# Expert tiles of a routed MLP: gate and up products ordered high rows first, and a tile's result copied from PSUM by ScalarE

## Chip, cores and metric

One core of one Trainium2 chip runs the whole program. The metric is the device time of one execution in microseconds (us). A change of less than about 0.2% cannot be told from no change here.

## What is computed

The model has two layers. Layer 0 is an attention and a dense MLP whose weights are made from splines; layer 1 is a selective scan followed by a mixture of experts. The change touches the expert part alone, which in the reference is:

```python
# D = 512, M = 192, 32 experts, 8 per token, T = 2048 tokens
routing_weights = jax.nn.softmax(x2d @ gate_kernel, axis=-1)
routing_weights, selected_experts = jax.lax.top_k(routing_weights, TOP_K)
routing_weights = routing_weights / jnp.sum(routing_weights, axis=-1, keepdims=True)
...
w0 = jax.lax.ragged_dot(sorted_inputs, gate_proj, group_sizes)
w1 = jax.lax.ragged_dot(sorted_inputs, up_proj, group_sizes)
inter = jax.nn.silu(w0) * w1
expert_out = jax.lax.ragged_dot(inter, down_proj, group_sizes)
...
output = jnp.einsum('BKE,BK->BE', per_token, routing_weights)
x = x + output
```

## The kernel before

Blocks A, B and C (up to about 1235 us) are attention, dense MLP, scan and routing. Block D (`block_d`) is the expert part. The 16384 token and expert pairs are sorted by expert and cut into tiles of 128 rows; an expert has 4 or 5 tiles, and block D works through some 144 tiles in order. The five engines each run their own loop over the tiles, unrolled by 8 (VectorE by 4), and meet only at semaphores. Every f32 operand is cut into a high part (rounded to fp32r) and a low part (the rest), and a product is made of high by high, high by low and low by high.

What happens to tile t:

- POOL (GpSimd) gathers its 128 rows from HBM with an indirect DMA (`D_rows<-rows_d`, L1458), four tiles ahead: in its turn for tile t it first issues the gather of tile t+4, and then the scatter of tile t (L1491), an indirect DMA that adds the tile's result to `out`. Two experts can add to one row of `out`. So at the first tile of each expert POOL waits, ahead of the scatter, until all scatters before it have landed. After every fourth tile it also copies four columns of indices (L1455).
- PE turns the rows (`turn_rows`, L1296, four transposes into one bank, `pT`). ScalarE copies that bank to `xT_hi` (`turn`, L1363, semaphore `xT_first`). VectorE then takes bank minus `xT_hi` as `xT_lo` (`turn_lo`, L1412, semaphore `xT_sb`).
- PE makes gate and up (`gate_up`, L1300 to L1302, 12 products for four chunks of 128 rows: for each chunk `xT_hi` by `W_gu_hi`, `xT_hi` by `W_gu_lo`, `xT_lo` by `W_gu_hi`).
- ScalarE makes silu (L1367), VectorE multiplies by up and by the token's share (`weigh`, L1405 and L1407, semaphore `inner_done`), PE turns that (L1336), VectorE cuts it in high and low (L1428, L1430), PE makes the five down products (L1352 to L1356), VectorE copies the sum from PSUM to `ysb` (`D_y`, L1444, semaphore `y_sb`), and POOL scatters it.

PE's turn for tile t is: the transposes L1336 of tile t, `gate_up` of tile t+1, `turn_rows` of tile t+2, the down products of tile t. Time from one L1336 to the next is called a PE turn below.

Once for each expert, three experts ahead (`SPLIT_AHEAD`), the weights are cut too: ScalarE makes `W_gu_hi` (L1370) and `W_d_hi` (L1210, L1211) at the end of its turn for the expert's first tile, and VectorE makes `W_gu_lo` (L1436) and `W_d_lo` (L1450) in its turn for the second tile, `W_gu_lo` ahead of `weigh` and `W_d_lo` at the end. Both have two SBUF inputs. When they are done SP loads the next expert's weights.

Of the kernel before, what the change touches and what calls it, by code (L numbers as in the profile page):

```python
# [16 lines left out]
ds = bass.ds  # L17
# [5 lines left out]
ACT = mybir.ActivationFunctionType  # L23
AX = mybir.AxisListType.X

P = 128
NB, L, D = 4, 512, 512
DC = 256
KC = D // P
# [12 lines left out]
GUW, MR = 2 * M, M - P  # L42
UNROLL = 8
# [3 lines left out]
NSLOT, NRAW = 4, 2  # L47
# [1175 lines left out]
def block_d(nc, a, X, ident, bank, meta, idx_all, W, rows_d):  # L1223

    with ExitStack() as s:
# [4 lines left out]
        xT_hi, xT_lo = ([sb(f"xT_{h}{i}", [P, KC * P], F32R) for i in range(2)] for h in ("hi", "lo"))  # L1230
        sil, inner = [sb(f"sil{i}", [P, M]) for i in range(2)], [sb(f"inner{i}", [P, 2 * P]) for i in range(2)]
        iT_hi, iT_lo = ([sb(f"iT_{h}{i}", [P, 2 * P], F32R) for i in range(2)] for h in ("hi", "lo"))
        ysb = sb("y", [P, UNROLL, D])
        first_counts = sb("first_counts", [1, 4])
        pT, piT, pgu, py = bank[0], bank[1], [bank[2], bank[3]], [bank[4], bank[5]]
# [3 lines left out]
        xT_ps, xT_first, xT_sb, gu_ps, sil_done, inner_done, iT_ps, iT_first, iT_sb, y_ps, y_sb = (  # L1239
            sem(n) for n in ("xT_ps", "xT_first", "xT_sb", "gu_ps", "sil_done", "inner_done", "iT_ps", "iT_first", "iT_sb", "y_ps", "y_sb"))  # L1240
# [3 lines left out]
        def field(eng, f, tile, hi):  # L1244

            return eng.value_load(meta[0:1, f, ds(tile, 1)], min_val=0, max_val=hi)
# [6 lines left out]
        def fetch(eng, regs, f, tile):  # L1253

            eng.load(regs, meta[0:1, f, ds(tile, len(regs))])  # L1255
# [5 lines left out]
        def ring(eng, e, ahead, size):  # L1261

            return eng.snap((e + ahead) & (size - 1), min_val=0, max_val=size - 1)
# [28 lines left out]
        @block.tensor  # L1292
        def _(pe):
            def turn_rows(i):
                for k in range(KC):
                    mm = pe.transpose(pT[:, k * P:(k + 1) * P], rows[i][:, k * P:(k + 1) * P], ident[:, :])  # L1296
                mm.then_inc(xT_ps, 1)

            def split_products(ps, hi, lo, whi, wlo, n, last):
                pe.matmul(ps, hi, whi, start=n == 0, stop=False)  # L1300
                pe.matmul(ps, hi, wlo, start=False, stop=False)  # L1301
                return pe.matmul(ps, lo, whi, start=False, stop=last)  # L1302

            def gate_up(buf, i, meanwhile=None):
                for k in range(KC):
                    if k == 2 and meanwhile:
                        meanwhile()
                    x, w = slice(k * P, (k + 1) * P), slice(k * GUW, (k + 1) * GUW)
                    whi, wlo = (t[:, ds(buf, 1), w].rearrange("p o n -> p (o n)") for t in (W.gu_hi, W.gu_lo))
                    mm = split_products(pgu[i % 2][:, 0:GUW], xT_hi[i % 2][:, x], xT_lo[i % 2][:, x], whi, wlo, k, k == KC - 1)  # L1310
                mm.then_inc(gu_ps, 1)

            pe.wait_ge(ld_rows[0], 16)
            turn_rows(0)
            buf = field(pe, SLOT, 0, NSLOT - 1)
            pe.wait_ge(W.gu_split, 1)
            pe.wait_ge(xT_sb, 1)
            gate_up(buf, 0)
            pe.wait_ge(ld_rows[1], 16)
            turn_rows(1)  # L1320


            experts, go = registers(pe, "pe_experts", UNROLL), pe.alloc_register("pe_go")
            fetch(pe, [go], GO, 0)
            fetch(pe, experts[0:HALF], EXPERT, 0)
            with pe.Fori(0, NTILE // UNROLL) as q:
                with pe.If(held(pe, go, 1) > 0):
                    ahead = {0: lambda: fetch(pe, experts[HALF:], EXPERT, q * UNROLL + HALF),
                             2: lambda: fetch(pe, [go], GO, q * UNROLL + UNROLL),
                             HALF: lambda: fetch(pe, experts[:HALF], EXPERT, q * UNROLL + UNROLL)}  # L1330
                    for i in range(UNROLL):
                        t = q * UNROLL + i
                        expert, next_expert = (held(pe, experts[n % UNROLL], NE - 1) for n in (i, i + 1))
                        pe.wait_ge(inner_done, t + 1)
                        for c in range(2):
                            mm = pe.transpose(piT[:, c * P:(c + 1) * P], inner[i % 2][:, c * P:(c + 1) * P], ident[:, :])  # L1336
                        mm.then_inc(iT_ps, 1)

                        pe.wait_ge(xT_sb, t + 2)
                        pe.wait_ge(W.gu_split, next_expert + 1)  # L1340
                        gate_up(ring(pe, next_expert, 0, NSLOT), i + 1, ahead.get(i))

                        j = (i + 2) % UNROLL
                        pe.wait_ge(ld_rows[j], q * 16 + (16 if i + 2 < UNROLL else 32))
                        turn_rows(j)
                        pe.wait_ge(iT_sb, t + 1)
                        pe.wait_ge(W.d_split, expert + 1)
                        buf = ring(pe, expert, 0, NSLOT)
                        first, last = slice(0, P), slice(P, 2 * P)
                        hi_a = W.d_hi[:, ds(buf, 1), 0:D].rearrange("p o n -> p (o n)")  # L1350
                        lo_a, both_b = (W.d_lo[:, ds(buf, 1), c * D:(c + 1) * D].rearrange("p o n -> p (o n)") for c in range(2))
                        pe.matmul(py[i % 2][:, :], iT_hi[i % 2][:, first], hi_a, start=True, stop=False)  # L1352
                        pe.matmul(py[i % 2][:, :], iT_lo[i % 2][:, first], hi_a, start=False, stop=False)
                        pe.matmul(py[i % 2][:, :], iT_hi[i % 2][:, first], lo_a, start=False, stop=False)
                        pe.matmul(py[i % 2][:, :], iT_hi[i % 2][:, last], both_b, start=False, stop=False)
                        mm = pe.matmul(py[i % 2][:, :], iT_lo[i % 2][:, last], both_b, start=False, stop=True)  # L1356
                        mm.then_inc(y_ps, 1)

        @block.scalar
        def _(act):  # L1360
            def turn(n, i):
                act.wait_ge(xT_ps, n + 1)
                act.activation(xT_hi[i % 2][:, :], pT[:, :], ACT.Copy).then_inc(xT_first, 1)  # L1363

            def silu(n, i):
                act.wait_ge(gu_ps, n + 1)
                act.activation(sil[i % 2][:, :], pgu[i % 2][:, 0:M], ACT.Silu).then_inc(sil_done, 1)  # L1367

            def split_hi(raw, buf):
                act.activation(slot(W.gu_hi, buf), slot(W.raw_gu, raw), ACT.Copy).then_inc(W.gu_hi_done, 1)  # L1370
                W.split_down_hi(act, raw, buf).then_inc(W.d_hi_done, 1)

            turn(0, 0)
            silu(0, 0)
            turn(1, 1)
            splits, go = registers(act, "act_splits", UNROLL), act.alloc_register("act_go")
            fetch(act, [go], GO, 0)
            fetch(act, splits, SPLITS, 0)
            with act.Fori(0, NTILE // UNROLL) as q:
                with act.If(held(act, go, 1) > 0):  # L1380
                    to_split = [held(act, r, 1) for r in splits]
                    for i in range(UNROLL):
                        t = q * UNROLL + i
                        if i == 2:
                            fetch(act, [go], GO, q * UNROLL + UNROLL)
                        if i == HALF:
                            fetch(act, splits, SPLITS, q * UNROLL + UNROLL)
                        silu(t + 1, i + 1)
                        turn(t + 2, i + 2)
                        with act.If(to_split[i] > 0):  # L1390
                            e = field(act, EXPERT, t, NE - 1 - SPLIT_AHEAD)
                            act.wait_ge(W.ld, (e + SPLIT_AHEAD + 1) * 32)
                            act.sem_inc(passed)
                            split_hi(ring(act, e, SPLIT_AHEAD, NRAW), ring(act, e, SPLIT_AHEAD, NSLOT))

        @block.vector
        def _(v):
# [24 lines left out]
            with v.Fori(0, NTILE // HALF) as q:  # L1422
                with v.If(held(v, go, 1) > 0):
                    code = [held(v, r, NE - 1 + CODE_SHARE * NE) for r in codes]
                    for i in range(HALF):
                        t = q * HALF + i
# [4 lines left out]
                        with v.If(code[i] > CODE_SHARE - 1):  # L1431
                            e1 = v.snap(code[i] >> CODE_BITS, min_val=1, max_val=NE - SPLIT_AHEAD)
                            raw, buf = ring(v, e1, SPLIT_AHEAD - 1, NRAW), ring(v, e1, SPLIT_AHEAD - 1, NSLOT)
# [6 lines left out]
                            fetch(v, codes, CODE, q * HALF + HALF)  # L1440
                        if i == 2:
                            fetch(v, [go], GO, ((q + 1) >> 1) * UNROLL)
                        v.wait_ge(y_ps, t + 1)
                        v.tensor_copy(ysb[:, ds(t & (UNROLL - 1), 1), :].rearrange("p o n -> p (o n)"), py[i % 2][:, :]).then_inc(y_sb, 1)  # L1444
                        with v.If(code[i] > CODE_SHARE - 1):
                            e1 = v.snap(code[i] >> CODE_BITS, min_val=1, max_val=NE - SPLIT_AHEAD)
                            raw, buf = ring(v, e1, SPLIT_AHEAD - 1, NRAW), ring(v, e1, SPLIT_AHEAD - 1, NSLOT)
# [101 lines left out]
```

## Time and profile before

| what | value |
|---|---|
| median of three runs | 1982.0 us (1979.49 to 1982.53) |
| profiled execution | 1981.46 us, span 1979.3 us |
| PE busy | 1614.6 us, 82% of the span |
| VectorE (DVE) busy | 1205.5 us, 61% |
| POOL busy | 1132.2 us, 57% |
| ScalarE (ACT) busy | 787.1 us, 40% |
| block D, 1236 to 1966 us | 730 us: PE 633.9, DVE 465.6, POOL 412.4, ACT 215.2 us busy |

Busy time counts an engine's own work. PE's matmuls overlap, so that their summed durations say little about how fast they follow each other; the starts in the timeline do. Waits on a semaphore are shown as idle time with what ended it.

### The profile page before, as it was taken

Reading aid. Unit: us, or ns where it says so; the run is one execution under the profiler, and the core shown is the slowest. Engines: PE = TensorE matmul, PEld = TensorE weight load, DVE = VectorE, ACT = ScalarE, POOL = GpSimd, SP = SyncE. Lnnn points to the kernel's source line nnn. Section 1 sums busy time; section 2 is a strip of 40 time slices with the busy share of each in tenths; the row PEclk is TensorE's granted clock in tenths of the full one; section 3 lists DMA queues with packets and bytes.
Section 4 is the critical chain, followed back from the end, with each engine's and each line's share of the span. In section 5 each row is a group of like instructions: output and inputs, shape, how many; then the busy total and the mean of one; then the engine's idle time right before and its main releaser. Section 6 shows DMA issues by size and latency. Waiting matters only on the chain. (4 is left out here: it accounts for less than half of the span.)

```text
span 1979.3 us, 24590 instructions
## 1 busy us (share of the span) xinstructions
PE 1614.6 (82%) x5970; PEld 997.9 (50%) x5971; DVE 1205.5 (61%) x2202; ACT 787.1 (40%) x1131; POOL 1132.2 (57%) x573
## 2 busy tenths in 40 slices
PE   5887758999999999899993553888888888888896
PEld 2333333444444444444441542777777777776775
DVE  3655675566565655565656568566656666665664
ACT  3344435555555555555553610332222232223221
POOL 0211128888888878887981221466555556555564
PEclk9878878999999999999996655999999999999998
DMA  3122226667666766675768421677767677776665
GB/s 118 75 75 75 90 98 181 136 139 157 165 137 135 157 156 144 135 163 127 147 123 248 121 74 55 150 169 178 168 157 164 160 157 159 183 178 150 152 116 97
DMA packets 78787, 275.73 MB, mean 139 GB/s; under 512 B 11266, under 2 KB 12195, under 8 KB 66963
## 3 DMA queue, kind: packets, MB, share of 16 engines
q0 software_dynamic: 42496, 150.37, 38.6%
q1 hardware_dynamic: 36242, 124.79, 20.0%
q8 instruction: 21, 0.34, 0.1%
q14 instruction: 28, 0.22, 0.0%
HBM read 148.22 MB, written 126.90 MB: 139 GB/s over the span
## 5 line engine op out<-in xcount | busy, mean ns | idle before, releaser
L690 DVE TENSOR_TENSOR_SCAN B_E<-bank,B_E 128x512 f32<-128x512 f32 x256 | 306.5, 1212 | 205.4 <-ACT bank L645 199.2
L1491 POOL DMA_INDIRECT out_x<-D_y,D_rows x144 | 253.0, 1757 | 224.0 <-issue 117.1
L733 POOL TENSOR_TENSOR B_E<-B_E,B_Cb 128x2048 f32<-128x2048 f32 x64 | 291.9, 4561 | 109.7 <-DVE B_E L690 109.7
L727 POOL TENSOR_TENSOR B_E<-B_dtu,B_Bb 128x2048 f32<-128x2048 f32 x64 | 292.3, 4567 | 31.6 <-DMA B_Bb<-bc_d 31.6
L1300 PE MATMUL bank<-W_gu_hi,D_xT_hi 128*128 x580 | 213.8, 369 | 62.5 <-DVE D_xT_lo L1412 60.7
L606 PE MATMUL bank<-B_Wd,B_inter 128*128 128x512 f32 x512 | 230.7, 597 | 33.3 <-DVE X L684 32.4
L596 PE MATMUL bank<-hT,B_Wg 128*128 128x512 f32 x512 | 235.5, 603 | 22.3 <-DVE B_inter L679 21.2
L596 PE MATMUL bank<-hT,B_Wu 128*128 128x512 f32 x512 | 230.2, 592 | 0.0
L645 ACT ACTIVATE bank<-B_dtv,negA 128x512 f32<-128x512 f32 x256 | 171.8, 687 | 136.4 <-DVE B_E L690 135.7
L1367 ACT ACTIVATE D_sil<-bank 128x192 f32<-128x192 f32 x145 | 47.9, 330 | 446.7 <-PE bank L1302 446.6
L1458 POOL DMA_INDIRECT D_rows<-rows_d,D_source x148 | 159.1, 1075 | 98.5 <-issue 92.0
L1301 PE MATMUL bank<-W_gu_lo,D_xT_hi 128*128 x580 | 197.3, 340 | 0.0
L1302 PE MATMUL bank<-W_gu_hi,D_xT_lo 128*128 x580 | 197.0, 340 | 0.0
L1405 DVE SCALAR_TENSOR_TENSOR D_inner<-D_sil,D_rows,bank 128x128 f32<-128x128 f32 x145 | 50.3, 347 | 200.3 <-ACT D_sil L1367 200.1
L606 PEld LDWEIGHTS bank<-B_Wd,B_inter 128*128 128x128 f32 x512 | 92.8, 190 | 155.7 <-issue 91.9
L596 PEld LDWEIGHTS bank<-hT,B_Wg 128*128 128x128 f32 x512 | 97.0, 193 | 142.4 <-issue 140.6
L1300 PEld LDWEIGHTS bank<-W_gu_hi,D_xT_hi 128*128 128x128 f32 x580 | 110.6, 191 | 99.3 <-issue 98.5
L596 PEld LDWEIGHTS bank<-hT,B_Wu 128*128 128x128 f32 x512 | 97.4, 190 | 122.3 <-issue 122.3
L1363 ACT ACTIVATE D_xT_hi<-bank 128x512 fp32r<-128x512 f32 x146 | 87.4, 599 | 111.9 <-PE bank L1296 98.8
L1412 DVE TENSOR_TENSOR D_xT_lo<-bank,D_xT_hi 128x512 fp32r<-128x512 f32 x146 | 100.0, 685 | 32.0 <-ACT D_xT_hi L1363 32.0
L1296 PE MATMUL bank<-ident,D_rows 128*128 128x128 f32 x584 | 89.8, 277 | 35.3 <-DMA D_rows<-rows_d,D_source 35.2
L364 POOL TENSOR_SCALAR A_one<-A_ex 128x2048 f32<-128x2048 f32 x4 | 21.5, 5367 | 169.3 <-ACT A_ex L279 169.3
(244 smaller groups left out, 2838.5 us busy)
## 6 DMA issues: line engine op xcount, KB each, us to landing
y_d<-B_E POOLq DMA_DIRECT2D x64, 1024.0 KB, 8.1
W_raw_gu<-in_wgu SPq DMA_DIRECT2D x32, 768.0 KB, 6.1
B_Bb<-bc_d SPq DMA_DIRECT2D x32, 512.0 KB, 5.4
B_Cb<-bc_d SPq DMA_DIRECT2D x32, 512.0 KB, 4.0
W_raw_d<-in_wd SPq DMA_DIRECT2D x32, 512.0 KB, 7.5
rows_d<-C_row SPq DMA_DIRECT2D x4, 1090.0 KB, 5.1
X<-in_x SPq DMA_DIRECT2D x4, 1024.0 KB, 9.0
dt_d<-A_dtv SPq DMA_DIRECT2D x4, 1024.0 KB, 3.9
```

The costliest lines, as they stand in the source:

```text
L596: mm = pe.matmul(ps[:, :], W[:, k, ch * P:(ch + 1) * P], hT[:, k, tb * L:(tb + 1) * L], start=k == 0, stop=k == KC - 1)
L606: mm = pe.matmul(Yb[t % 2][:, :], inter[jj % 2][:, ch, t * P:(t + 1) * P], Wd[w][:, ch, :], start=ch == 0, stop=ch == 1)
L645: act.activation(dA[m % 2][:, :], dtv[:, c, :], ACT.Exp, scale=negA[:, c, n:n + 1]).then_inc(dA_done, 1)
L690: v.tensor_tensor_scan(E[:, s % NR, c, :], dA[m % 2][:, :], E[:, s % NR, c, :], 0.0, ALU.mult, ALU.add).then_inc(s_done, 1)
L727: g.tensor_tensor(E[:, s % NR, :, :], dtu[b % 2][:, :, :], spread(Bb[jj % 2][:, s % 2, :]), ALU.mult).then_inc(dbu_done, 1)
L733: g.tensor_tensor(E[:, s % NR, :, :], E[:, s % NR, :, :], spread(Cb[jj % 2][:, s % 2, :]), ALU.mult).then_inc(prod_done, 1)
L1300: pe.matmul(ps, hi, whi, start=n == 0, stop=False)
L1301: pe.matmul(ps, hi, wlo, start=False, stop=False)
L1302: return pe.matmul(ps, lo, whi, start=False, stop=last)
L1412: v.tensor_tensor(xT_lo[i % 2][:, :], pT[:, :], xT_hi[i % 2][:, :], ALU.subtract).then_inc(xT_sb, 1)
L1458: g.indirect_dma_start(rows[i], None, rows_d[:, :], bass.IndirectOffsetOnAxis(ap=source[i // HALF][:, i % HALF:i % HALF + 1].bitcast(U32), ...
L1491: g.indirect_dma_start(a["out"], bass.IndirectOffsetOnAxis(ap=rows[i][:, ROW - 1:ROW].bitcast(U32), axis=0), ysb[:, i, :], None, compute_o ...
```

## The change

`gate_up` makes the eight products with `xT_hi` first, all four chunks, and then the four with `xT_lo`. It waits for `xT_first` ahead of the first eight and for `xT_sb` only ahead of the last four. The reading of registers that stood in the middle of it (`meanwhile`) stands between the two halves. The copy of a tile's result from PSUM leaves VectorE's turn, where it stood behind `turn_lo`, and goes to ScalarE's turn, behind `turn` and ahead of the cutting of weights.

```diff
-            def split_products(ps, hi, lo, whi, wlo, n, last):
-                pe.matmul(ps, hi, whi, start=n == 0, stop=False)
-                pe.matmul(ps, hi, wlo, start=False, stop=False)
-                return pe.matmul(ps, lo, whi, start=False, stop=last)
-
-            def gate_up(buf, i, meanwhile=None):
+
+            def gate_up(buf, i, tile, meanwhile=None):
+                ps = pgu[i % 2][:, 0:GUW]
+
+                def operands(k, x, w):
+                    return x[i % 2][:, k * P:(k + 1) * P], w[:, ds(buf, 1), k * GUW:(k + 1) * GUW].rearrange("p o n -> p (o n)")
+                pe.wait_ge(xT_first, tile + 1)
                 for k in range(KC):
-                    if k == 2 and meanwhile:
-                        meanwhile()
-                    x, w = slice(k * P, (k + 1) * P), slice(k * GUW, (k + 1) * GUW)
-                    whi, wlo = (t[:, ds(buf, 1), w].rearrange("p o n -> p (o n)") for t in (W.gu_hi, W.gu_lo))
-                    mm = split_products(pgu[i % 2][:, 0:GUW], xT_hi[i % 2][:, x], xT_lo[i % 2][:, x], whi, wlo, k, k == KC - 1)
+                    pe.matmul(ps, *operands(k, xT_hi, W.gu_hi), start=k == 0, stop=False)
+                    pe.matmul(ps, *operands(k, xT_hi, W.gu_lo), start=False, stop=False)
+                if meanwhile:
+                    meanwhile()
+                pe.wait_ge(xT_sb, tile + 1)
+                for k in range(KC):
+                    mm = pe.matmul(ps, *operands(k, xT_lo, W.gu_hi), start=False, stop=k == KC - 1)
                 mm.then_inc(gu_ps, 1)
...
-                        pe.wait_ge(xT_sb, t + 2)
                         pe.wait_ge(W.gu_split, next_expert + 1)
-                        gate_up(ring(pe, next_expert, 0, NSLOT), i + 1, ahead.get(i))
+                        gate_up(ring(pe, next_expert, 0, NSLOT), i + 1, t + 1, ahead.get(i))
...
                         turn(t + 2, i + 2)
+                        act.wait_ge(y_ps, t + 1)
+                        act.activation(ysb[:, i, :], py[i % 2][:, :], ACT.Copy).then_inc(y_sb, 1)
                         with act.If(to_split[i] > 0):
...
-                        v.wait_ge(y_ps, t + 1)
-                        v.tensor_copy(ysb[:, ds(t & (UNROLL - 1), 1), :].rearrange("p o n -> p (o n)"), py[i % 2][:, :]).then_inc(y_sb, 1)
```

PE's queue in a tile's turn before, from the transposes of `inner` to the second chunk of `gate_up` (REGISTER_ALU and ISA rows are the sequencer's work on addresses, and the semaphore a row waits for is in brackets):

```order
L1336 MATMUL bank<-ident,D_inner 128x128 [waits D_inner_done]
L1336 MATMUL bank<-ident,D_inner 128x128
L1339 REGISTER_ALU
L1340 REGISTER_ALU [waits D_xT_sb]
L1300 REGISTER_ALU [waits W_gu_split]
L1300 ISA
L1300 MATMUL bank<-W_gu_hi,D_xT_hi 128x384
L1301 REGISTER_ALU
L1301 MATMUL bank<-W_gu_lo,D_xT_hi 128x384
L1302 MATMUL bank<-W_gu_hi,D_xT_lo 128x384
```

The same place after the change, with the end of `gate_up` behind the "...":

```order
L1338 MATMUL bank<-ident,D_inner 128x128 [waits D_inner_done]
L1338 MATMUL bank<-ident,D_inner 128x128
L1341 REGISTER_ALU
L1305 REGISTER_ALU [waits W_gu_split]
L1307 REGISTER_ALU [waits D_xT_first]
L1307 ISA
L1307 MATMUL bank<-W_gu_hi,D_xT_hi 128x384
L1308 REGISTER_ALU
L1308 MATMUL bank<-W_gu_lo,D_xT_hi 128x384
...
L1255 TENSOR_LOAD meta
L1313 MATMUL bank<-W_gu_hi,D_xT_lo 128x384 [waits D_xT_sb]
```

The wait for `D_xT_sb` has moved behind eight products and the register load; the number of products and of sequencer rows ahead of the first product is what it was.

ScalarE's queue in a tile's turn after the change, from silu to the cutting of the gate and up weights:

```order
L1368 ACTIVATE D_sil<-bank 128x192 [waits D_gu_ps]
L1363 REGISTER_ALU
L1364 ACTIVATE D_xT_hi<-bank 128x512 [waits D_xT_ps]
L1391 REGISTER_ALU
L1392 ACTIVATE D_y<-bank 128x512 [waits D_y_ps]
L1393 COMPARE_AND_BRANCH
L1246 ISA
L1246 TENSOR_LOAD meta
L1246 ISA x2
L1395 ISA
L1371 REGISTER_ALU [waits W_ld]
```

The two rows with L1391 and L1392 are new; ahead of the branch there stood nothing between it and the copy to `D_xT_hi`. The register load `L1246` and all of the weight cutting now come behind a wait for PE's down products.

## Rows read from the trace of the kernel before

**Rows 1.** Window, block D; busy (count) of PE, PEld, DVE, ACT, POOL; granted clock.
```profile
1236.00:1966.00 730.00, 633.89 (x3328) 523.03 (x3328) 465.60 (x928) 215.18 (x382) 412.42 (x321) 0.99 0.70 158
```

**Rows 2.** Waits in 1236 to 1966 us: total, times, longest.
```profile
PE bank L1300 <- DVE D_xT_lo L1412: 60.7, 139, 1.6
PE bank L1296 <- DMA D_rows<-rows_d,D_source: 25.8, 18, 2.9
```

**Rows 3.** Timeline of a plain tile: start us, us, engine, line, names.
```profile
1606.10 0.68 DVE L1412 TENSOR_TENSOR D_xT_lo<-bank,D_xT_hi 128x512 fp32r<-128x512 f32 x1
1606.23 0.44 PE L1336 MATMUL bank<-ident,D_inner 128*128 128x128 f32 x2
...
1606.70 0.68 DVE L1444 COPY D_y<-bank 128x512 f32 x1
1607.12 0.44 PE L1300 MATMUL bank<-W_gu_hi,D_xT_hi 128*128 x1 [0.44 <-DVE D_xT_lo L1412]
...
1608.22 1.58 POOL L1491 DMA_INDIRECT out_x<-D_y,D_rows  x1 [1.75 <-DVE D_y L1444]
...
1609.31 0.60 PE L1296 MATMUL bank<-ident,D_rows 128*128 128x128 f32 x4
...
1610.95 0.44 PE L1336 MATMUL bank<-ident,D_inner 128*128 128x128 f32 x2
```

**Rows 4.** Timeline behind a long wait for rows.
```profile
1423.29 2.40 POOL L1491 DMA_INDIRECT out_x<-D_y,D_rows  x1 [3.01 <-issue]
...
1428.00 1.01 POOL L1458 DMA_INDIRECT D_rows<-rows_d,D_source  x1 [2.11 <-issue]
...
1435.19 1.12 PE L1296 MATMUL bank<-ident,D_rows 128*128 128x128 f32 x4 [2.41 <-DMA D_rows<-rows_d,D_source]
...
1438.23 0.39 PE L1336 MATMUL bank<-ident,D_inner 128*128 128x128 f32 x2
...
1438.38 0.42 PE L1300 MATMUL bank<-W_gu_hi,D_xT_hi 128*128 x1
...
1442.19 0.44 PE L1336 MATMUL bank<-ident,D_inner 128*128 128x128 f32 x2
```

**Rows 5.** Groups of instructions by line, 1236 to 1966 us.
```profile
L1363 ACT ACTIVATE D_xT_hi<-bank 128x512 fp32r<-128x512 f32 x146 | 87.4, 599 | 111.9 <-PE bank L1296 98.8
L1211 ACT ACTIVATE W_d_hi<-W_raw_d x30 | 18.9, 629 | 0.4
```

**Rows 6.** One line, L1436: durations, first and last start.
```profile
L1436 DVE TENSOR_TENSOR W_gu_lo<-W_raw_gu,W_gu_hi x30: 1757/1758/1761, 1249.3 to 1901.0; - x30
```

**Rows 7.** Timeline of an expert's four tiles around its first scatter.
```profile
1327.92 1.59 POOL L1491 DMA_INDIRECT out_x<-D_y,D_rows  x1 [0.81 <-DVE D_y L1444]
...
1330.73 1.49 ACT L1370 ACTIVATE W_gu_hi<-W_raw_gu  x1 [0.63 <-issue]
...
1333.49 1.76 DVE L1436 TENSOR_TENSOR W_gu_lo<-W_raw_gu,W_gu_hi  x1 [0.35 <-issue]
...
1333.72 2.98 POOL L1491 DMA_INDIRECT out_x<-D_y,D_rows  x1 [2.91 <-issue]
...
1336.88 1.22 DVE L1450 TENSOR_TENSOR W_d_lo<-W_raw_d,W_d_hi  x1
1337.01 1.96 POOL L1458 DMA_INDIRECT D_rows<-rows_d,D_source  x1 [0.30 <-DVE D_y L1444]
...
1344.45 0.66 PE L1296 MATMUL bank<-ident,D_rows 128*128 128x128 f32 x4 [0.64 <-DMA D_rows<-rows_d,D_source]
...
1348.04 1.59 POOL L1491 DMA_INDIRECT out_x<-D_y,D_rows  x1 [1.00 <-DVE D_y L1444]
```

**Rows 8.** Timeline of another expert's first scatter.
```profile
1465.54 1.49 ACT L1370 ACTIVATE W_gu_hi<-W_raw_gu  x1 [1.19 <-issue]
1467.35 1.58 POOL L1491 DMA_INDIRECT out_x<-D_y,D_rows  x1 [3.05 <-issue]
1467.60 1.76 DVE L1436 TENSOR_TENSOR W_gu_lo<-W_raw_gu,W_gu_hi  x1 [0.69 <-ACT W_gu_hi L1370]
```

More of the change, by code:

```diff
@@ L1316, in _ @@
             pe.wait_ge(W.gu_split, 1)
-            pe.wait_ge(xT_sb, 1)
-            gate_up(buf, 0)
+            gate_up(buf, 0, 0)
             pe.wait_ge(ld_rows[1], 16)
```

## The prediction

> **What bounds the kernel now.** I read the windows first. Block D takes 730 us, and PE, busy 634 us of them, is the fullest engine at full clock (0.99) [rows 1]; only this block is changed. Then the waits. PE waits for two things: `xT_lo` from VectorE, 139 times, 60.7 us in all, and gathered rows, 18 times, 25.8 us [rows 2]. So there are two limits, and I followed each in the timeline.
>
> The first is PE's own turn. In a plain tile it is 1610.95 - 1606.23 = 4.72 us. `turn_lo` ends at 1606.78, `gate_up` starts at 1607.12, 0.89 us after L1336 [rows 3], and the engine is idle 0.44 us of that. At 1438.23 rows had been late, so that `xT_lo` was long there: `gate_up` starts 0.15 us after L1336, and the turn is 1442.19 - 1438.23 = 3.96 us [rows 4].
>
> The second is a loop that runs once per expert through POOL. Take S1 at 1327.92 (the last scatter of the old expert) and S2 at 1333.72 (the first of the new one): 5.80 us, the time S1 needs to land. S2 takes 2.98 us where an undisturbed one takes 1.59, because `W_gu_lo` runs on VectorE from 1333.49 to 1335.25: S2 ends 1.45 us after it. The gather behind S2 starts at 1337.01, inside `W_d_lo` (1336.88 to 1338.10), and takes 1.96 us against 1.01. Its rows land 7.4 us after its start, and PE had waited 0.64 us for them at 1344.45; the down products behind them feed the scatter at 1348.04, the next S1 [rows 7, 4]. That is 20.12 us for four tiles, where PE alone would need 4 x 4.72 plus about 0.5 for the turn that `W_gu_lo` delays, 19.4. The loop and PE's work are nearly equally long. Where the index copy falls between S2 and the gather, the gather starts 4.71 us after S2 (1423.29 to 1428.00), PE waits 2.41 us, and the cycle is some 22.3 us [rows 4]; by the numbers of the tiles at which experts start in the timeline (modulo 4) this is so in 9 of 29 cycles.
>
> `W_gu_lo` runs 30 times, from 1249.3 to 1901.0 [rows 6]: 29 cycles of 22.47 us with 129 tiles, 4.45 a cycle.
>
> **The change, part by part.**
>
> (a) The early start of `gate_up`. `xT_hi` is ready 0.9 us before `xT_lo`, always ahead of L1336, so the wait goes. But the rows of PE's queue between L1336 and the first product stay, and the sequencer stands at `inner_done` until VectorE is through. From `xT_lo`'s end to the first product these rows now take 0.34 us [rows 3]; the bound below is 0.15, where the sequencer had run ahead [rows 4]. I take 0.40, nearer the plain tile: a saving of 0.49 a turn, 4.72 to 4.23. The bound is 0.74, 3.98. Twelve products take 1609.31 - 1607.12 = 2.19 us [rows 3], the eight high ones so 1.46, in which `xT_lo` is ready: its wait costs nothing.
>
> (b) The copy of the result. VectorE loses 144 copies of 0.68 us [rows 3]. The nearest form on ScalarE, also 128x512 from PSUM, takes 0.599 [rows 5]; the last down product stands right ahead of the next L1336 in PE's queue, and I put its end 0.15 us behind that one's start (an estimate; matmuls overlap). So the copy is done at 0.15 + 0.05 + 0.60 = 0.8 us of the turn, against 1.15 (1607.38 - 1606.23 [rows 3]) for VectorE. In a plain turn ScalarE is idle then; nothing is delayed. In the loop this is worth about 0.25 us a cycle.
>
> (c) In the turn in which weights are cut, ScalarE's work comes later. `W_gu_hi` starts 0.63 us behind the end of the instruction ahead [rows 7], now the copy: at 0.8 + 0.63 = 1.4 us of the turn instead of 0.2. It ends at 2.9, the two parts of `W_d_hi` (0.62 and 0.63) at 4.2 [rows 7, 5], and silu of the next tile, due at 2.8, waits for it. `W_gu_lo` starts 0.57 behind `W_gu_hi`'s end when it waits for it (1467.03 to 1467.60 [rows 8]): 3.5 to 5.25. `weigh` follows, and this turn becomes about 5.8 us, where it was 5.3. So PE alone needs 5.8 + 3 x 4.23 = 18.5 us for four tiles.
>
> (d) What becomes of the loop? In [rows 7] S2 started 0.23 us after `W_gu_lo` and stood until it ended. In [rows 8] S2 started 0.25 us before it and took 1.58: whichever starts first is not held up. The Trainium skill (SBUF — State Buffer, Who interferes with whom) says the same: a VectorE instruction with two SBUF inputs contends with GpSimd's reads, and the order of issue decides who blocks; by that rule the moved copy, which reads PSUM, never held POOL up. Here the order can turn over. S1 starts at 0.8 + 0.84 = 1.64 us of its turn (0.84 from `D_y`'s end at 1607.38 to its scatter at 1608.22 [rows 3]), S2 5.8 to 5.9 us later, which is 3.3 us of the following turn after 4.23 are taken off; `W_gu_lo` starts at 3.5. S2 is first by 0.2 us, less than these numbers are sure to. If S2 is first, it ends 1.4 us sooner than now, the gather is 2.3 us sooner done, and the loop falls to about 17.6, below PE's 18.5: PE bounds most experts. With the index copy behind S2 it is about 19.8. If `W_gu_lo` is first, the gather is done 1.75 + 1.05 + 0.9 behind it as now or 0.5 sooner, and the loop is 20.12 - 0.25 - 0.3 = about 19.55, with the index copy 22.3.
>
> The sum over 29 cycles of 4.45 tiles. S2 first: 18.5 + 0.45 x 4.23 + 9/29 x 1.3 = 20.8, a gain of 1.65 a cycle, 48 us. `W_gu_lo` first: 19.55 + 1.9 + 9/29 x 2.8 = 22.3, a gain of 0.15, 4 us. Ahead of the first cutting and behind the last there are 15 tiles more; POOL's drains bound most, and I take 4 us. With S2 first in two of three experts: 0.67 x 48 + 0.33 x 4 + 4 = 37 or 38. From the profiled 1981.46 that is 1944; the median, 1982.0, gives the same to 1 us.
>
> **The rivals.** *One: `W_gu_lo` meets every S2.* For it: it does in nearly all experts now, and my margin is 0.2 us. Gain 4 + 4: 1974, or up to 1980 if rows land later under the denser traffic (DMA share is 0.70 already [rows 1]). *Two: PE gets the whole 0.74 us*, the sequencer runs ahead, and S2 is first everywhere: 5.8 + 3 x 3.98 = 17.7 for four tiles, 17.7 + 1.8 + 9/29 x 2.1 = 20.2 a cycle, 29 x 0.6 = 17 us beyond the full gain of 48 + 4: 1912 or, with 3 us at the ends, 1909. Against it: the wait at `inner_done` ends just as the down products do. With 3.98 S2 also comes 0.25 later in its turn, beside `W_gu_lo`, so this needs luck twice. *Three, slower.* A PE that finishes sooner waits longer for the same rows. Behind the wait of 2.41 us its clock was low: four transposes took 1.12 us in place of 0.66, and L1336 came 3.04 us after their start where 1.64 is usual [rows 4, 7, 3]: the lower of the two levels, 1.4 us in the loop itself. If rival one holds and PE's waits of 1 us grow to 2.4 in more than 6 of 29 cycles (8 / 1.4), the gain of 8 is gone; in 21 of them, counting off the ones that have it now, it is 1974 + 30 = 2004. Against it: the plain cycle's wait would be 19.55 - 18.5 = 1.05 us. *Four: the delayed silu costs more than its 0.5 us*, because transposes of later rows queue behind it; that is the same loss by another way, inside the range of rival one.
>
> **How the numbers follow.** S2 first in most experts, forecast 1944 (own range 1928 to 1962): 0.45. Rival one, 1974 (1964 to 1982): 0.25. Rival two, 1905 to 1926: 0.13. Slower, to 2004: 0.13. A remainder of 0.04 on either side. The range that leaves out no more than 2 in 10: 1912 to 1984. Faster by over 0.2% (about what a measurement can tell, below 1978): 0.45 + 0.13 + 0.19 of rival one = 0.77. Within 0.2%: 0.09. Slower: 0.14.
>
> **What would show it.** (a) No wait of the first product for VectorE, and plain turns of 4.2 us from L1336 to L1336; 4.0 is rival two. (b) `D_y` on ScalarE, about 0.60. (c) `W_gu_hi` 1.4 us into its turn, and a turn of 5.8. (d) The durations of the scatters: now most expert starts show 1.8 to 3.1 us; near 1.58 in two thirds says S2 first, 3.0 in all says rival one. In rival three the down products behind waits for rows last twice as long. I am wrong if rows land much later than 7.4 us, or if the first scatter's place in the turn is off by more than 0.2 us.

## The result, and the profile after

The kernel after takes 1948.5 us (median of 4, 1946.3 to 1950.6) against 1980.7 us before on the same chip (median of 4): ratio 0.984, 95% interval 0.982 to 0.986. The forecast was 1944. The profiled execution took 1950.59 us with a span of 1948.8.

Block D's window, with the columns of [rows 1]:

```profile
1236.00:1966.00 730.00, 634.18 (x3332) 535.87 (x3331) 380.69 (x784) 295.41 (x526) 402.02 (x326) 0.96 0.71 159
```

VectorE is down from 466 to 381 us and ScalarE up from 215 to 295, as the moved copy should do. The window reaches past the end of this shorter run (span 1948.8), so the clock is better compared over 1236 to 1910 us: it is 0.96, where the kernel before has 0.98 (short parts of the block are at the lower level, 1.2 GHz, the rest at 2.4). The waits of the same stretch, with the columns of [rows 2], and behind them PE's wait for `D_inner` in the kernel before:

```profile
DVE W_gu_lo L1439 <- ACT W_gu_hi L1371: 63.1, 30, 2.6
PE bank L1338 <- DVE D_inner L1410: 50.8, 31, 2.1
PE bank L1296 <- DMA D_rows<-rows_d,D_source: 17.7, 10, 9.6
PE bank L1307 <- ACT D_xT_hi L1364: 0.9, 1, 0.9
```
```profile
PE bank L1336 <- DVE D_inner L1407: 5.6, 12, 0.8
```

The 139 waits of PE for `xT_lo` are gone. The wait for `D_inner`, 5.6 us in all before, is now about 1.6 us once per expert. The wait for rows seems to fall from 25.8 to 17.7 us, but 9.6 of the 17.7 is the one at the block's start. The kernel before has that one too, 9.4 us at 1234.5, which is just outside the window of [rows 2]. Like for like it is 18 waits and 25.8 us before, 9 waits and 8.1 us after. A plain tile, as in [rows 3]:

```profile
1612.02 0.44 PE L1338 MATMUL bank<-ident,D_inner 128*128 128x128 f32 x2
1612.18 0.60 ACT L1392 ACTIVATE D_y<-bank 128x512 f32<-128x512 f32 x1 [0.57 <-PE bank L1357]
1612.40 0.44 PE L1307 MATMUL bank<-W_gu_hi,D_xT_hi 128*128 x1
...
1613.62 1.58 POOL L1492 DMA_INDIRECT out_x<-D_y,D_rows  x1 [1.02 <-ACT D_y L1392]
...
1614.62 0.60 PE L1296 MATMUL bank<-ident,D_rows 128*128 128x128 f32 x4
...
1616.24 0.44 PE L1338 MATMUL bank<-ident,D_inner 128*128 128x128 f32 x2
```

The turn is 1616.24 - 1612.02 = 4.22 us (4.72 before), and the first product comes 0.38 us behind L1338 (0.89 before). The copy as a group (us in all, mean ns), and the line of `W_gu_lo`, as in [rows 6]:

```profile
L1392 ACT ACTIVATE D_y<-bank 128x512 f32<-128x512 f32 x144 | 86.3, 599 | 69.1 <-PE bank L1357 69.1
```
```profile
L1439 DVE TENSOR_TENSOR W_gu_lo<-W_raw_gu,W_gu_hi x30: 1757/1759/1853, 1251.1 to 1872.5; - x30
```

29 cycles now take 1872.5 - 1251.1 = 621.4 us, 21.4 each, where they took 22.5: 30 of the 32 us. An expert's four tiles, as in [rows 7]:

```profile
1327.31 1.59 POOL L1492 DMA_INDIRECT out_x<-D_y,D_rows  x1 [0.54 <-issue]
...
1331.39 1.49 ACT L1371 ACTIVATE W_gu_hi<-W_raw_gu  x1 [0.73 <-issue]
...
1333.25 1.58 POOL L1492 DMA_INDIRECT out_x<-D_y,D_rows  x1 [3.04 <-issue]
...
1333.46 1.76 DVE L1439 TENSOR_TENSOR W_gu_lo<-W_raw_gu,W_gu_hi  x1 [1.44 <-ACT W_gu_hi L1371]
...
1335.13 1.00 POOL L1459 DMA_INDIRECT D_rows<-rows_d,D_source  x1 [0.31 <-issue]
...
1335.79 0.44 PE L1338 MATMUL bank<-ident,D_inner 128*128 128x128 f32 x2 [1.84 <-DVE D_inner L1410]
...
1342.57 0.60 PE L1296 MATMUL bank<-ident,D_rows 128*128 128x128 f32 x4
...
1346.41 1.59 POOL L1492 DMA_INDIRECT out_x<-D_y,D_rows  x1 [0.30 <-issue]
```

S2 starts 0.21 us ahead of `W_gu_lo` and takes 1.58 us; the gather is done 8.8 us behind S1 where before it was 11.1, and PE turns its rows at 1342.57 without a wait. S1 to S1' is 19.1 us (20.1 before). Over the block S2 is first in 24 of 30 experts, and scatters of over 1.7 us are down from 28 to 12. `W_gu_hi` starts 1.4 to 2.0 us into its turn; that turn's median is 5.95 us.

What the forecast did not have is the turn behind it. Two windows on that place, with the columns above, and the start of the first one's turn:

```profile
1511.40:1517.20 5.80, 5.75 (x23) 5.17 (x24) 3.74 (x7) 0.93 (x2) 4.88 (x4) 0.71 0.66 122
1622.00:1626.60 4.60, 4.46 (x24) 3.73 (x25) 3.59 (x8) 0.93 (x2) 3.08 (x3) 1.00 0.85 140
```
```profile
1511.44 0.44 PE L1338 MATMUL bank<-ident,D_inner 128*128 128x128 f32 x2 [1.68 <-DVE D_inner L1410]
...
1512.97 0.51 PE L1307 MATMUL bank<-W_gu_hi,D_xT_hi 128*128 x1
...
1513.59 1.48 PE L1313 MATMUL bank<-W_gu_hi,D_xT_lo 128*128 x4
```

Both follow a wait for `D_inner` of 1.5 to 1.7 us. In the first the clock falls to the lower level (0.71 on average), four low products take 1.48 us where 0.87 is usual, and the turn takes 5.76 us. The second keeps 1.00 and takes 4.5. Of the 30 turns behind a cutting turn (the turn in which `W_gu_lo` runs) 12 had a granted clock of 0.70 or 0.71 and took 5.55 to 5.80 us. The other 18 were at 1.00; one of them took 5.11 us and one 4.98, and in both PE's down products waited 0.5 to 0.6 us for VectorE.

### The profile page after: what moved, and what is told of

It reads as the page before. It is cut to its first block and busy times, and to the rows that moved or that the text cites. A ratio compares the mean times of both kernels' runs of the same rounds, so it can differ in the third digit from the quotient of the medians.

```text
span 1948.8 us, 24428 instructions
## 1 busy us (share of the span) xinstructions
PE 1614.4 (83%) x5970; PEld 1009.8 (52%) x5971; DVE 1120.6 (58%) x2058; ACT 866.9 (44%) x1275; POOL 1118.4 (57%) x573
## 5 line engine op out<-in xcount | busy, mean ns | idle before, releaser
L1492 POOL DMA_INDIRECT out_x<-D_y,D_rows x144 | 240.1, 1668 | 205.2 <-issue 108.2
L596 PE MATMUL bank<-hT,B_Wg 128*128 128x512 f32 x512 | 237.1, 607 | 22.6 <-DVE B_inter L679 21.5
L1459 POOL DMA_INDIRECT D_rows<-rows_d,D_source x148 | 155.1, 1048 | 99.9 <-issue 97.0
L1308 PE MATMUL bank<-W_gu_lo,D_xT_hi 128*128 x580 | 201.9, 348 | 0.0
L1313 PE MATMUL bank<-W_gu_hi,D_xT_lo 128*128 x580 | 132.4, 353 | 0.5 <-issue 0.5
L364 POOL TENSOR_SCALAR A_one<-A_ex 128x2048 f32<-128x2048 f32 x4 | 21.5, 5367 | 168.9 <-ACT A_ex L279 168.9
L1392 ACT ACTIVATE D_y<-bank 128x512 f32<-128x512 f32 x144 | 86.3, 599 | 69.1 <-PE bank L1357 69.1
L1308 PEld LDWEIGHTS bank<-W_gu_lo,D_xT_hi 128*128 128x128 f32 x580 | 113.2, 195 | 0.0
```

Source lines behind the costliest of these rows:

```text
L596: mm = pe.matmul(ps[:, :], W[:, k, ch * P:(ch + 1) * P], hT[:, k, tb * L:(tb + 1) * L], start=k == 0, stop=k == KC - 1)
L1308: pe.matmul(ps, *operands(k, xT_hi, W.gu_lo), start=False, stop=False)
L1313: mm = pe.matmul(ps, *operands(k, xT_lo, W.gu_hi), start=False, stop=k == KC - 1)
L1459: g.indirect_dma_start(rows[i], None, rows_d[:, :], bass.IndirectOffsetOnAxis(ap=source[i // HALF][:, i % HALF:i % HALF + 1].bitcast(U32), ...
L1492: g.indirect_dma_start(a["out"], bass.IndirectOffsetOnAxis(ap=rows[i][:, ROW - 1:ROW].bitcast(U32), axis=0), ysb[:, i, :], None, compute_o ...
```

## The experiments

Most of these kernels are the one after with an edit; the one with the copy alone and one of those with rows five tiles ahead are the kernel before with an edit, and the text says so there. All have masks (`& (NE - 1)`) on register values from which the waits for semaphores and the addresses of weights are made. "Control" is the kernel after with the masks and nothing else, and the others are to be compared with it. Ratios are to the kernel before on the same chip, with the 95% interval in brackets. The kernel before took 1976.8 us on the chip of the control, the halves and the filled wait, 1980.3 on that of the four kernels with a changed cutting turn, 1977.6 on that of the first three with rows five tiles ahead and 1981.3 on that of the last, so that a difference in us between these groups is sure to some 4 us only. I grouped PE's turns by place: the one in which `W_gu_lo` runs (cut), the one behind it (next), the second behind it (second, in which the rows gathered behind S2 are first used with four tiles ahead), and the others; values are means worked out from the starts of L1338 (or its line in that kernel). A cycle is the time from one `W_gu_lo` to the next.

**Control.** `experts[...]` and `code[i] >> CODE_BITS` gain `& (NE - 1)`.

> The changed kernel with its register values masked (a few sequencer operations on PE ahead of the wait for inner_done, and three on VectorE ahead of the waits for cut weights), as the later variants have them. Both theories: no visible cost, 1945 to 1952 us, plain turns of 4.22 us, most first scatters of an expert at 1.58 us.

1946.1 us, 0.984 (0.982 to 0.985). Turns: cut 5.98, next 4.81, second 4.46, others 4.20; cycle 21.3 us. The masks cost nothing. Of the turns behind the cutting one 7 are at the lower clock here, for 12 in the kernel after.

**One half at a time.** With the products alone the copy is back on VectorE, behind `turn_lo`:

```diff
-                        act.wait_ge(y_ps, t + 1)
-                        act.activation(ysb[:, i, :], py[i % 2][:, :], ACT.Copy).then_inc(y_sb, 1)
+                        v.wait_ge(y_ps, t + 1)
+                        v.tensor_copy(ysb[:, ds(t & (UNROLL - 1), 1), :].rearrange("p o n -> p (o n)"), py[i % 2][:, :]).then_inc(y_sb, 1)
```

> High rows first, the copy of the result stays on VectorE. My theory (the order of the first scatter and W_gu_lo decides): W_gu_hi starts 0.2 us into its turn, W_gu_lo at 2.3 to 3.0, the first scatter at 3.6, so that it is held up in nearly every expert (1.8 to 3.1 us) and the POOL loop bounds: 1960 us, 1950 to 1970, slower than the whole change although PE's turns are as short. Rival (PE's work bounds, the collision doesn't matter): the turn in which weights are cut is shorter, 4.7 instead of 5.8 us, and there is no low clock behind it, so 30 x 1.1 us better than the whole change: 1900 to 1925 us.

1949.2 us, 0.987 (0.983 to 0.991), 11 us less than the 1960 of the expectation and just outside its range. Turns: cut 4.91, next 4.72, second 5.75, others 4.20; 23 scatters over 1.7 us. The cutting turn is 1.1 us shorter than the control's, and the second behind it 1.3 us longer. With the copy alone (the kernel before with the copy on ScalarE):

> The copy on ScalarE, products in the old order. My theory: plain turns stay 4.7 us, the turn with cut weights becomes about 6, the first scatter of an expert comes ahead of W_gu_lo and is free; PE's work, 20.1 us for four tiles, takes the loop's place: 1974 us, 1965 to 1985. Rival (the copy relieves VectorE and POOL, and that is the gain): clearly faster, below 1960 us.

1973.6 us, 0.998 (0.997 to 1.000). Turns: cut 5.82, next 4.86, second 4.63, others 4.70; no S2 is held up. So the products bring 28 us, the copy 3, and together they bring 31: the two halves add up. By the turns the copy takes 1.2 us from the second turn behind (5.80 before) and puts 0.8 us on the cutting turn (4.98 before).

**The wait behind the cutting turn, filled.** PE makes ten transposes into an unused bank there. The output does not change. Only the added transposes are shown; PE also reads the code of the tile in place of the expert, to know where to make them.

```diff
+                        with pe.If(held(pe, experts[i], NE - 1 + CODE_SHARE * NE) > CODE_SHARE - 1):
+                            for n in range(FILL):
+                                pe.transpose(bank[6][:, (n % KC) * P:(n % KC + 1) * P], ident[:, :], ident[:, :])
```

> The changed kernel plus ten transposes of the identity into an unused PSUM bank, on PE ahead of the wait for inner_done in the turn in which W_gu_lo is made (1.1 us of work inside a wait of 1.5 to 1.9 us). Theory that the idle wait lowers the clock in the turn behind it: the 11 turns of 5.76 us behind that turn become 4.2 to 4.8 us, the granted clock of block D stays near 1.00, and the kernel gains 8 to 17 us on the control: 1932 to 1941 us. Rival (those turns are long for late rows or for W_d_lo, or the low clock has another cause): no gain or a loss of up to 5 us for the branches, 1947 to 1955 us.

1942.1 us, 0.981 (0.980 to 0.983). Its window of the 29 cycles:

```profile
1236.00:1910.00 674.00, 638.60 (x3544) 539.04 (x3543) 372.93 (x765) 289.09 (x514) 389.07 (x315) 1.00 0.73 168
```

The clock is 1.00 (control 0.98), and the turn behind falls from 4.81 to 4.55 us. None of the turns behind is at the lower clock (7 in the control). The 4.55 that are left stay 0.35 above a plain turn, at full clock. In 9 of these 30 turns PE's down products wait 0.3 to 0.7 us (4.3 us in all) for `iT_lo`, which VectorE makes behind `W_d_lo`; this is about 0.15 of the 0.35. And the second one behind grows from 4.46 to 4.66: 0.20 of the 0.26 us come back, in the turn that is first to use the rows gathered behind S2. The kernel gained 4 us where 8 to 17 were looked for, and the intervals of the two ratios overlap.

**The cutting turn made shorter.** If PE alone bounds, this pays; it did not, three times. First the copy behind all cutting (its two lines leave their place ahead of the `If`):

```diff
                         with act.If(to_split[i] > 0):
                             ...
                             split_hi(ring(act, e, SPLIT_AHEAD, NRAW), ring(act, e, SPLIT_AHEAD, NSLOT))
+                        act.wait_ge(y_ps, t + 1)
+                        act.activation(ysb[:, i, :], py[i % 2][:, :], ACT.Copy).then_inc(y_sb, 1)
```

> ScalarE copies the result behind all of the weight cutting. The first scatter of an expert gets its data at 3.6 + 0.84 = 4.4 us of the turn instead of being ready at 3.3, behind W_gu_lo (2.3 to 4.05), and takes 1.58. Loop theory: the loop grows by the 1.1 us, 19.2 to 19.5 us for four tiles, and the shorter turn (5.0 instead of 5.95) gives nothing: 1950 us, 1943 to 1960. Rival (PE bounds): 1920 us or below.

1985.0 us, 1.003 (1.001 to 1.005), slower than before. Its loop, and its waits for rows:

```profile
1329.34 1.59 POOL L1495 DMA_INDIRECT out_x<-D_y,D_rows  x1 [1.02 <-ACT D_y L1400]
...
1336.23 1.58 POOL L1495 DMA_INDIRECT out_x<-D_y,D_rows  x1 [4.00 <-ACT D_y L1400]
...
1338.12 1.61 POOL L1462 DMA_INDIRECT D_rows<-rows_d,D_source  x1 [0.30 <-issue]
...
1345.81 0.66 PE L1296 MATMUL bank<-ident,D_rows 128*128 128x128 f32 x4 [2.00 <-DMA D_rows<-rows_d,D_source]
```
```profile
PE bank L1296 <- DMA D_rows<-rows_d,D_source: 80.1, 32, 9.4
```

S2 now waits for the late copy, not for the drain: 6.9 us behind S1 in place of 5.9. It is never held up (no scatter over 1.7 us). The gather starts 8.8 us behind S1 instead of 7.8, and PE waits 2.0 us for its rows. The cutting turn is 4.93 us, the second behind it 7.02.

Then `W_gu_hi` alone ahead of the copy, `W_d_hi` behind it (in tiles without cutting the copy stays behind `turn`):

```diff
                             act.activation(slot(W.gu_hi, buf), slot(W.raw_gu, raw), ACT.Copy).then_inc(W.gu_hi_done, 1)
+                            act.wait_ge(y_ps, t + 1)
+                            act.activation(ysb[:, i, :], py[i % 2][:, :], ACT.Copy).then_inc(y_sb, 1)
                             W.split_down_hi(act, raw, buf).then_inc(W.d_hi_done, 1)
```

> In the turn in which weights are cut, ScalarE makes W_gu_hi ahead of the copy of the result and W_d_hi behind it. Both theories: W_gu_hi at 0.2 us, W_gu_lo at 2.3, silu at 3.6 instead of 4.2, the turn 5.1 instead of 5.95 us. Theory that the POOL loop bounds as soon as W_gu_lo is ahead of the first scatter (3.3): the scatter takes 2.3, the gather behind it meets W_d_lo, four tiles take 19.2 us and nothing is gained: 1950 us, 1942 to 1958. Rival (PE's and ScalarE's work bounds): 30 x 0.85 us, 1920 us or below.

1965.6 us, 0.993 (0.992 to 0.995). The same places:

```profile
1331.55 1.59 POOL L1502 DMA_INDIRECT out_x<-D_y,D_rows  x1 [0.80 <-ACT D_y L1407]
...
1336.49 1.76 DVE L1449 TENSOR_TENSOR W_gu_lo<-W_raw_gu,W_gu_hi  x1 [0.46 <-issue]
...
1337.43 2.29 POOL L1502 DMA_INDIRECT out_x<-D_y,D_rows  x1 [2.98 <-issue]
...
1340.02 1.64 POOL L1469 DMA_INDIRECT D_rows<-rows_d,D_source  x1 [0.30 <-issue]
```

`W_gu_lo` is now first, S2 ends 1.47 us behind it, and the gather starts 8.5 us behind S1. Cut 4.90, second behind 6.10. Both kernels traded 1.1 us of the cutting turn for more than that at the rows.

Not every expert pays. The copy of indices (`D_source<-idx_all`) stands between S2 and its gather for some of them, as here in this kernel, with S1 at 1415.68, and the gather then starts 10.7 us behind S1:

```profile
1421.54 1.99 POOL L1502 DMA_INDIRECT out_x<-D_y,D_rows  x1 [2.97 <-issue]
1422.96 1.59 POOL L1466 COPY D_source<-idx_all 128x4 int32 x1
1426.40 1.01 POOL L1469 DMA_INDIRECT D_rows<-rows_d,D_source  x1 [1.86 <-issue]
```

I sorted the 28 full experts by this, and took the time from one S1 to the next (means in us, number of experts in brackets):

| kernel | 4 tiles, no index copy (10) | 4 tiles, index copy (6) | 5 tiles, no index copy (9) | 5 tiles, index copy (3) |
|---|---|---|---|---|
| before | 19.61 | 22.14 | 24.48 | 25.89 |
| after | 19.36 | 19.69 | 23.73 | 24.07 |
| control | 19.34 | 19.55 | 23.63 | 23.93 |
| `W_gu_hi` ahead of the copy | 19.02 | 21.58 | 23.16 | 27.72 |
| copy behind all cutting | 19.76 | 22.87 | 24.07 | 27.75 |

With `W_gu_hi` ahead of the copy the 19 experts without an index copy are 0.3 to 0.5 us shorter than the control's, 7 us in all; the 9 with one are 2.0 and 3.8 us longer, 24 us in all. So the whole loss sits in these 9. With the copy behind all cutting, 31 of the 39 us do. Of the gain of the change itself, two thirds (20 of 30 us) come from the same 9.

The other two attempts move `W_d_lo` into VectorE's turn of the next tile, with this kernel and with the control:

> As the one before, and VectorE makes W_d_lo in the next tile's turn, behind the cutting of inner. Loop theory: the gather behind the first scatter no longer meets W_d_lo (about 1.0 instead of 1.9 us), four tiles take 18.2 us by the loop and 17.8 by PE: 1931 us, 1924 to 1940. Rival (W_d_lo's place doesn't matter): within 3 us of the kernel with only W_gu_hi moved.

1958.9 us, 0.990 (0.988 to 0.991), 28 us above the expectation. Cut 4.91, next 4.38, second 5.16; 49 scatters over 1.7 us, the expert's second scatter is often held up too (19 of 29).

> The changed kernel with W_d_lo in the next tile's turn. It shows whether the down products that waited for VectorE behind W_d_lo (0.5 to 0.9 us in some eight turns behind the one with cut weights) and the 14 to 22 gathers that met it cost anything: if so 1938 to 1943 us; if these waits are hidden by the next wait for rows, 1944 to 1948.

1961.7 us, 0.991 (0.989 to 0.993), 16 us slower than the control, where no loss was looked for. Cut 5.99, next 4.67, second 4.19, others 4.68 (control 4.20). PE's waits for rows in 1236 to 1910 us:

```profile
PE bank L1296 <- DMA D_rows<-rows_d,D_source: 29.1, 17, 9.6
```

Besides the one at the block's start, all 16 stand in the third turn behind the cutting one, 19.5 us in all; the control has 2 there, 0.8 us in all. These rows are gathered behind the expert's second scatter. That scatter is now over 1.7 us in 11 of 29 experts (5 in the control), the gather behind it is held up in 9 (none in the control), and it is done 0.7 us later on average, counted from S1.

**Slack for the loop.** If the rows' due time is the other bound, asking for them one tile sooner must pay, and then so must a shorter cutting turn. The eight row buffers allow it: the gather for tile t+5 needs the scatter of tile t-3 landed. The edit also moves the index copy one tile earlier, so that it stands between S2 and its gather for 5 of the 28 experts and no longer for 9; no kernel has that move alone.

```diff
-                        g.wait_ge(added[i % 4], done)
-                        gather((i + HALF) % UNROLL)
+                        g.wait_ge(added[(i + 1) % 4], 32 * q + 16 * ((i + 1) // 4 + 1))
+                        gather((i + HALF + 1) % UNROLL)
...
-                        if i % HALF == HALF - 1:
-                            take((i // HALF + 2) % 2, t + (HALF + 1))
+                        if i % HALF == HALF - 2:
+                            take((i // HALF + 2) % 2, t + (HALF + 2))
```

> The control with rows gathered five tiles ahead in place of four, and the index copy one tile earlier; PE's and ScalarE's work is what it was. Theory: once per expert the loop through POOL (last scatter of the old expert, its landing, first scatter, gather, rows, next expert's last scatter) sets the end, and PE waits for rows at its end. Rows that are asked for one tile sooner give this loop 4.2 us of slack, so PE's own turns are left: 5.95 + 3 x 4.22 = 18.6 us for four tiles, 20.5 a cycle of 4.45 tiles where the control takes 21.34, and 29 x 0.84 = 24 us: 1922 us (1912 to 1932), the wait for rows near zero behind the block's first tiles, few turns at the lower clock. Rival: PE's own turns bound already and the waits are by the way: 1940 to 1950.

1926.6 us, 0.974 (0.972 to 0.976). Window and waits:

```profile
1236.00:1910.00 674.00, 619.40 (x3330) 517.86 (x3328) 378.93 (x784) 295.98 (x526) 398.25 (x326) 1.00 0.76 172
```
```profile
DVE W_gu_lo L1442 <- ACT W_gu_hi L1374: 56.3, 30, 2.5
PE bank L1341 <- DVE D_inner L1413: 47.7, 31, 1.9
```

No wait of PE for rows is left in it. Turns: cut 5.91, next 4.45, second 4.17, others 4.23; cycle 20.7 us (20.5 expected). Scatters are held up about as often as in the control (13 over 1.7 us, for 10), and it costs nothing now. The slack pays without the index copy too: the four-tile experts without one take 18.79 us where the control's take 19.34. PE's waits for `D_inner` come to nearly the same sum as in the kernel after (47.7 for 50.8 us), yet no turn is at the lower clock.

The kernel before, with rows gathered five tiles ahead:

> The kernel before with rows gathered five tiles ahead. Its plain turn is 4.72 us, its cutting turn about 5.0 and the one behind it 4.9, so PE alone needs 4.45 x 4.72 + 0.6 = 21.6 a cycle where it took 22.47: a gain of 25 us, 1955 us (1945 to 1965), if the loop through POOL was one of its two bounds. Then the change as a whole would be worth 30 us beside the slack, as it is without it. If PE's turn alone bounded it: 1972 to 1980.

1953.0 us, 0.987 (0.985 to 0.988). Nearly every expert's S2 is held up there, as here:

```profile
1335.50 1.76 DVE L1439 TENSOR_TENSOR W_gu_lo<-W_raw_gu,W_gu_hi  x1 [0.45 <-issue]
...
1335.71 3.00 POOL L1494 DMA_INDIRECT out_x<-D_y,D_rows  x1 [2.98 <-issue]
...
1339.02 1.96 POOL L1461 DMA_INDIRECT D_rows<-rows_d,D_source  x1 [0.30 <-DVE D_y L1447]
```

and still the second turn behind is 4.67 us where it was 5.80 before: a scatter of 3.0 us costs only where rows are due. The cycle is 21.4 us. With that slack the change is worth 1953.0 - 1926.6 = 26 us.

The kernel that makes `W_gu_hi` ahead of the copy, with rows gathered five tiles ahead:

> As the kernel that makes W_gu_hi ahead of the copy (cutting turn 4.8 us in place of 5.95), with rows gathered five tiles ahead. Theory: a shorter cutting turn gained nothing because the loop through POOL had no slack; with slack it should pay 29 x 1.1 = 32 us on top of the gather five tiles ahead: 1890 us (1880 to 1905). Rival: W_gu_lo and W_d_lo on VectorE hold up scatters and gathers and that costs PE by itself, whatever the slack: within 8 us of the kernel with five tiles ahead alone, 1915 to 1930, or slower than it.

1897.4 us, 0.959 (0.958 to 0.961), the fastest of all. `W_gu_hi` ahead of the copy, a loss of 19 us without slack (1965.6 against 1946.1), gains 29 us with it. Its waits:

```profile
PE bank L1341 <- DVE D_inner L1420: 15.2, 30, 0.8
PE bank L1296 <- DMA D_rows<-rows_d,D_source: 9.3, 1, 9.3
```

The one wait for rows is that at the block's start. Cut 4.85, next 4.53, second 4.20, others 4.23. The four-tile experts without an index copy take 17.70 us (19.02 with four tiles ahead), and 24 scatters are over 1.7 us.

The same with `W_d_lo` in VectorE's turn of the next tile:

> As the kernel with W_gu_hi ahead of the copy and rows five tiles ahead (1897 us), and W_d_lo in VectorE's turn of the next tile. Without the slack that move lost nothing against the same kernel (1959 against 1966), with 49 scatters over 1.7 us. Theory: with slack the held-up scatters cost PE nothing, and the turn behind the cutting one falls from 4.53 to 4.23 us on average, 30 x 0.3 = 9 us: 1888 us (1883 to 1895). Rival: the scatters and gathers that W_d_lo holds up eat the slack of one tile: above 1900, with waits for rows.

1897.6 us, 0.957 (0.956 to 0.959), the same as the kernel above, where 9 us were looked for. The next turn fell to 4.36 (4.23 expected), but the cutting turn and the two others rose by 0.02 to 0.07 us each and took it back.

## Why the prediction came out right, and where it did not

(a) **The early start of `gate_up`: right.** 4.22 us a plain turn (4.23 forecast, bound 3.98), the wait for `xT_lo` gone. By the half-change this is nearly the whole gain, 28 of 31 us.

(b) **The copy: right.** 0.599 us, done 0.76 us into the turn (0.8 forecast).

(c) **The cutting turn: right, slightly small.** 6.02 us on average (5.98 in the control), median 5.95, for 5.8; `W_gu_hi` at 1.4 to 2.0. This is the copy's price: alone, the copy gained 3 us.

(d) **Who is first: right.** S2 in 24 of 30 (two thirds forecast), and by 0.21 us in the expert shown (0.2 forecast). Here the traces agree again with the Trainium skill (SBUF — State Buffer, Who interferes with whom), that the order of issue decides: 1.58 us for S2 0.21 us ahead of `W_gu_lo` in the kernel after, 2.29 us for one 0.94 us behind its start in the kernel with `W_gu_hi` ahead of the copy.

**The sum: two terms off that cancel.** With 0.8 of the experts S2-first my own terms give 0.8 x 20.8 + 0.2 x 22.3 = 21.1 us a cycle, a gain of 39 us; measured are 21.4 and 30. The turn behind the cutting one was taken at 4.23 us and is 4.94: +0.7 a cycle. The cutting turn is +0.2. On the other side, PE's own turns make 5.8 + 3.45 x 4.23 = 20.4 of the 21.1, so that I had 0.7 for waits at the rows, and the second turn behind shows 4.42 - 4.22 = 0.2: -0.5. The three make 21.5. That the total came out within 5 us of the forecast is in part luck. The same shows by the kind of expert. For four tiles with the index copy the prediction had 19.8 us when S2 is first and 22.3 when it is not, and the kernels after and before have 19.69 and 22.14. Without the index copy it had 18.5, and the kernel after takes 19.36.

The nearest rival in kind was the third, PE at the lower clock behind a wait. It did occur, but behind the wait for `D_inner` that the change itself made, in 12 of 30 turns. These 12 are 18 us longer in all than as many plain turns, of the 22 us by which all 30 are longer, so that the clock took a part of the gain and not all. The rest of the 22 us is at full clock, most of it in 3 turns where the down products wait for VectorE. The filled wait shows the same: no turn at the lower clock, and still 4.55 us on average. What the clock is worth to the whole time is not shown, since filling gave only 4 us.

**What the prediction had as two limits is shown.** Slack for rows alone gave 20 us, a shorter cutting turn alone lost 19, both together gained 49. The expectations for the shorter cutting turns had the loop, but not the index copy, which the prediction had as a term of its own. They forecast 19.2 us for four tiles (`W_gu_hi` ahead of the copy) and 19.2 to 19.5 (copy behind all cutting). Without the index copy 19.02 and 19.76 were measured, with it 21.58 and 22.87. The times were 16 and 35 us above the expectations.

**Open.** Why the clock falls behind some waits for `D_inner` and not behind others. Their length is a part of it, but not all. In the kernel after the 12 turns at the lower clock follow waits of 1.58 to 2.07 us; 7 waits as long, and all 11 shorter ones, were followed by full clock. With rows five tiles ahead only 7 of the 30 waits are that long, and none was followed by the lower clock. A wait for rows stands some turns ahead of some of the slow turns, but not of all, so I name no cause. Open as well is how much of the gain with five tiles ahead is the moved index copy; that it is not all is shown by the experts without one.

## What to carry to other kernels

When two loops are nearly equally long, price an edit by what it does to each: here 1.1 us off PE's turn cost 19 us or brought 29, by whether rows were asked for four tiles ahead or five. And look at the cycles by kind before taking a mean: the loss sat in 9 of 28. Before shortening work in a loop, try whether asking for its input one step sooner removes a wait; it is a small edit and tells which loop binds. A wait moved to another place is to be priced at what follows it too, since the work behind it may run at the lower clock.

## What the runs showed of the hardware

An indirect scatter or gather issued on GpSimd during a VectorE subtraction with two SBUF inputs stands until that one has ended: scatters ended about 1.5 us behind it (S2 2.29 to 3.0 us for 1.58), gathers about 0.9 us behind it (1.61 to 1.96 us for 1.00). Issued ahead of it, it is not slowed: in the kernel after 31 scatters began ahead of such a subtraction and ran into it, and all took 1.58 or 1.59 us. Nor is one slowed that begins during `turn_lo`, whose inputs are one in PSUM and one in SBUF: 11 gathers in the kernel after took 1.00 to 1.01 us. Such a stand costs nothing by itself: with 30 scatters over 1.7 us the kernel before with five tiles ahead kept PE's own pace (4.72 us a plain turn). And a wait of 1.4 to 2.1 us on PE was followed by the lower clock in 12 of 30 cases in the kernel after and in 7 of 30 in the control, and in none of the 30 waits, 1.5 to 2.0 us long, of the kernel with five tiles ahead.
